# Vision transformer layer on one core: the wavelet tokeniser handled in pieces, with one gate chain and an inverse shared by three engines

## The reference, cut to what matters

```python
img = x[..., 0]                       # 8 images of 256 x 256
details, cur = [], img
for _ in range(3):                    # three Haar analysis levels
    cur, h, v, d = _dwt2(cur)
    details.append((h, v, d))
aw = sigmoid(cur.reshape(B, -1) @ Wa + ba)
rec = cur * aw[:, :, None]
for (h, v, d), (Wd, bd) in zip(reversed(details), [(Wd1, bd1), (Wd2, bd2), (Wd3, bd3)]):
    w = softmax(stack([h, v, d], 1).reshape(B, -1) @ Wd + bd, -1)     # 3 gates of a level
    rec = _idwt2(rec, h * w[:, 0], v * w[:, 1], d * w[:, 2])          # gates broadcast over a band
h = concatenate([cls_tok, rec], axis=1)         # an image row is a token: 257 tokens of 256
h = h + attention_block(layernorm(h))           # linear attention with 16 heads, then an MLP
h = h + moe(layernorm(h))                       # 8 experts, 2 per token
```

## Time and profile before

| what | value |
|---|---|
| median of three runs | 739.04 us (737.57 to 739.18) |
| the profiled execution | 734.85 us |
| its span, first to last instruction | 733.0 us |
| PE busy | 684.5 us, 93% |
| DVE / ACT / POOL busy | 47% / 40% / 39% |
| mean granted TensorE clock | 0.966 |

### The profile page before, as it was taken

How to read it: one execution, slowest core, us unless ns; L and a number is a source line. 1 busy time by engine, 2 the same in 40 slices (tenths; PEclk the granted TensorE clock), 3 DMA queues, 4 the chain that set the end, 5 groups by cost and what they waited for, 6 DMA issues and landing times.

```text
span 733.0 us, 14613 instructions
## 1 busy us (share of the span) xinstructions
PE 684.5 (93%) x4607; PEld 605.7 (83%) x4608; DVE 343.6 (47%) x1029; ACT 293.7 (40%) x762; POOL 289.1 (39%) x324
## 2 busy tenths in 40 slices
PE   0977999999999999999999999999999999999993
PEld 0755888889988877788888788999999999999993
DVE  5493766666532643654566554333333333333330
ACT  0432665466532363444345242333342424333330
POOL 7003677676662353444533332323232323232221
PEclk9978999999959999999999999999999999999997
DMA  9605999700000298011021253221221211122210
GB/s 210 221 2 97 271 303 307 207 0 1 2 0 1 82 377 289 16 45 45 23 81 59 96 183 94 37 43 30 44 34 30 34 34 30 30 36 37 36 22 0
DMA packets 53222, 63.97 MB, mean 87 GB/s; under 512 B 6348, under 2 KB 48768, under 8 KB 53008
## 3 DMA queue, kind: packets, MB, share of 16 engines
q1 hardware_dynamic: 41264, 50.61, 23.7%
q0 software_dynamic: 8112, 9.04, 7.4%
q10 hardware_dynamic: 3808, 3.82, 1.7%
HBM read 31.01 MB, written 31.38 MB: 85 GB/s over the span
## 4 chain that ended last, share of the span: by engine, by line
PE 73%; DVE 9%; SPq 5%; DMA 4%; issue 3%; ACT 2%; POOL 2%; DVEq 0%; POOLq 0%; ACTq 0%
PE bank L1702 70%; SPq L574 3%; DMA arena<-in_L_tok_Wa 2%; PE bank L2209 1%; DVE arena L1032 1%; DMA out_tokens<-h 1%; DMA h<-arena 1%; DVE small L549 1%; POOL small L570 1%; SPq L642 1%; PE bank L1734 1%; POOL arena L764 1%; PE bank L1880 1%; SPq L578 1%; DVE dense L562 1%
## 5 line engine op out<-in xcount | busy, mean ns | idle before, releaser
L1702 PE MATMUL bank<-arena,dense 128*128 (+2 forms) x1408 | 307.0, 389 | 1.1 <-ACT arena L1496 0.8
L1702 PEld LDWEIGHTS bank<-arena,dense 128*128 128x128 f32 (+1 forms) x1408 | 247.2, 193 | 37.1 <-ACT arena L1595 2.9
L1671 ACT ACTIVATE dense<-bank,small 128x128 f32<-128x128 f32 x320 | 91.1, 368 | 182.5 <-PE bank L1702 182.5
L857 POOL DMA_INDIRECT out_tokens<-dense,slot_ids x40 | 77.1, 1928 | 206.1 <-DVE dense L1415 197.4
L1702 PEld LDWEIGHTS bank<-dense 128*128 128x128 f32 x1280 | 149.0, 192 | 3.9 <-DVE dense L1393 2.0
L1702 PE MATMUL bank<-dense 128*128 128x128 f32 x1280 | 149.6, 275 | 1.6 <-DVE dense L1393 1.6
L1702 PE MATMUL bank<-dense,arena 128*128 128x256 f32 (+2 forms) x688 | 105.2, 352 | 1.1 <-ACT arena L1509 0.7
L764 POOL TENSOR_TENSOR arena<-arena 128x512 f32<-128x512 f32 x64 | 80.3, 1277 | 40.7 <-ACT arena L1529 40.7
L1702 PEld LDWEIGHTS bank<-dense,arena 128*128 128x128 f32 (+2 forms) x688 | 81.8, 186 | 16.3 <-issue 4.2
L1595 ACT ACTIVATE arena<-bank,small 128x256 f32<-128x256 f32 x128 | 53.7, 471 | 81.7 <-PE bank L1702 81.5
L1702 PE MATMUL bank<-arena 128*128 128x34 f32 (+7 forms) x756 | 81.8, 301 | 3.1 <-ACT arena L1595 1.6
(11 more groups left out here) (247 smaller groups left out, 580.1 us busy)
## 6 DMA issues: line engine op xcount, KB each, us to landing
routed_rows<-x SPq DMA_DIRECT2D x8, 2385.0 KB, 24.3
arena<-in_L_ffn_w SPq DMA_DIRECT2D x13, 1024.0 KB, 12.5
dense<-routed_rows SPq DMA_DIRECT2D x40, 132.5 KB, 2.1
arena<-in_L_ffn_w ACTq DMA_DIRECT2D x3, 1024.0 KB, 9.4
arena<-in_x SPq DMA_DIRECT2D x4, 512.0 KB, 7.0
arena<-in_L_attn_w SPq DMA_DIRECT2D x2, 1024.0 KB
out_tokens<-h SPq DMA_DIRECT2D x8, 256.0 KB, 2.2
h<-arena SPq DMA_DIRECT2D x13, 128.0 KB
```

The costliest lines, as they stand in the source:

```text
L857: pool.indirect_dma_start(out=sums[:, :], out_offset=bass.IndirectOffsetOnAxis(ap=slot_ids[par][:, 0:1], axis=0), in_=y[par], in_offset=No ...
L1671: act.activation(hT[par][:, k, :], psUP[par][c][:, P * m:P * m + P], ACT.Silu, bias=b1now[par][:, k:k + 1]).then_inc(hT_sb, 1)
L1702: return pe.matmul(out, lhsT, rhs, start=start, stop=stop, **kw)
```

## The change

- **Loads.** ACT's small loads and POOL's 16 wait for the image's last piece (`img_loaded[3]`). The weights of levels 1 and 2 come with 96 rows of half the length, so that one transpose turns two blocks; level 1's have a semaphore of their own.
- **Bands by piece.** DVE makes level 1's bands as each piece of the image arrives. PE turns them piece by piece, in eight units of three blocks, and multiplies in the order 1, 2, 3 of the levels. `picked` and the like are made after the analysis.
- **One gate chain.** `pick`, `total`, the logits and the exponentials are done once for all three levels, after the last dot product.
- **Inverse of level 1.** ACT multiplies the second and third band by their gates. POOL forms the high sums from them, in four instructions. DVE forms the low sums and interleaves, in two half strips of 8 rows, and raises `image_ready` after each.
- **Relayout.** A transfer takes 8 rows of each of an image's 16 strips. A token tile's partition p then holds another row of the image than before, and `ids` and the stores of `h` follow; a store becomes two. SP issues the first halves of images 0 to 2 after the first `image_ready`, then the second halves, then image 3. ACT issues those of images 4 to 7, behind its copies of the weights. POOL issues none.

```diff
@@ ACT, start
+            act.wait_ge(img_loaded[PIECES - 1], 16)
             for dst, src in smalls:
@@ POOL
+            pool.wait_ge(img_loaded[PIECES - 1], 16)
             for hh in range(HEADS):
...
-            pool.wait_ge(image_ready, 1)
-            for b in range(HELPED):
-                relay(pool, b, 1, helped[b])
+            pool.wait_ge(scaled, 2)
+            for part in range(2):
+                for r, op in ((0, ALU.add), (1, ALU.subtract)):
+                    ins = pool.tensor_tensor(hi4[:, 4 * part:4 * part + 4, r, :], level1(det[1][:, 1024:2048], part),
+                                             level1(det[1][:, 2048:3072], part), op)
+                ins.then_inc(hi_ready, 1)
+            pool.wait_ge(image_ready, 2)
@@ relay
-            p0 = STRIPS * b + STRIPS // T * j
-            eng.dma_start(h[:, T * b + j, :], img[p0:p0 + STRIPS // T, :].rearrange("p (r n) -> p r n", r=ROWS)
+            p0, c0 = STRIPS * b, RUN * IMG * j
+            eng.dma_start(h[:, T * b + j, :], img[p0:p0 + STRIPS, c0:c0 + RUN * IMG].rearrange("p (r n) -> p r n", r=RUN)
@@ SP
-            sp.wait_ge(image_ready, 1)
-            for b in range(B):
-                relay(sp, b, 0, relaid[min(b, 4)])
-                if b >= HELPED:
-                    relay(sp, b, 1, relaid[min(b, 4)])
+            for j in range(T):
+                sp.wait_ge(image_ready, j + 1)
+                for b in range(3):
+                    relay(sp, b, j, relaid[b])
+            for b in range(3, ON_SYNC):
+                for j in range(T):
+                    relay(sp, b, j, relaid[min(b, 4)])
...
-                sp.dma_start(sums[bass.ds(g * SEQ + 1, IMG), :].rearrange("(t p) n -> p t n", p=P),
-                             h[:, bass.ds(T * g, T), :]).then_inc(stored[par], 16)
+                for j in range(T):
+                    sp.dma_start(sums[bass.ds(g * SEQ + 1, IMG), :].rearrange("(s t r) n -> s t r n", s=STRIPS, t=T)[:, j, :, :],
+                                 h[:, bass.ds(T * g + j, 1), :].rearrange("p o n -> p (o n)")).then_inc(stored[par], 16)
@@ DVE
-            cur, side, rows = img, IMG, ROWS
-            for lvl in (1, 2, 3):
...
+            for i in range(PIECES):
+                dve.wait_ge(img_loaded[i], 16)
+                analyse(1, img, IMG, ROWS, i, PIECES)
...
-            pick(0)
-            logits_of(0, ((0, 3, 0.25), (4, 8, 0.125)), 2)
...
+            dve.wait_ge(dots_ps, 2)
+            for i in range(2):
+                ins = dve.tensor_tensor(dotted[:, i, :, :], psDots[i].rearrange("p (b s) -> p b s", s=STRIPS),
+                                        own.rearrange("p (o s) -> p o s", o=1).to_broadcast([P, B, STRIPS]), ALU.mult)
...
             link(merge(3))
-            pick(1)
             spread(2, 0, gsc[:, 12:13])
-            logits_of(1, ((0, 3, 0.5),), 1)
             link(merge(2))
             dve.wait_ge(c_ps, 1)
             dve.tensor_copy(c_xT, psT[:, 0:KD]).then_inc(c_done, 1)
...
-            spread(1, 8, gsc[:, 17:18])
-            merge(1).then_inc(image_ready, 1)
+            for part in range(2):
+                r0, m0 = 4 * part, 1024 * part
+                for r, g in ((0, gate[:, 8:9]), (1, gsc[:, 14:15])):
+                    ins = dve.scalar_tensor_tensor(out=rows4[:, r0:r0 + 4, r, :], in0=d0[:, r0:r0 + 4, :], scalar=g,
+                                                   in1=base[:, r0:r0 + 4, :], op0=ALU.mult, op1=ALU.add)
+                link(ins)
+                dve.wait_ge(hi_ready, part + 1)
+                for two, op in ((0, ALU.add), (1, ALU.subtract)):
+                    ins = dve.tensor_tensor(o2[:, m0:m0 + 1024, two], lohi[:, m0:m0 + 1024],
+                                            lohi[:, 2048 + m0:2048 + m0 + 1024], op)
+                ins.then_inc(image_ready, 1)
@@ ACT
+            act.wait_ge(gates_ready, 1)
+            for k in (1, 2):
+                d = det[1][:, 1024 * k:1024 * (k + 1)]
+                act.activation(d, d, ACT.Identity, scale=gate[:, 8 + k:9 + k]).then_inc(scaled, 1)
...
+            act.wait_ge(image_ready, 2)
+            for b in range(ON_SYNC, B):
+                for j in range(T):
+                    relay(act, b, j, relaid[4])
```

More of the change, by code:

```diff
@@ L52 @@
 TURNED_FIRST = 4
+RUN = ROWS // T
 BANDS = 3 * STRIPS
@@ L56 @@
 PIECES = 4
-HELPED = 3
+ON_SYNC = 4
 class Chain:
@@ new lines, in _ @@
+            levels = gate[:, 0:12].rearrange("p (l k) -> p l k", k=4)[:, :, 0:3]
+            dve.wait_ge(totals_ready, 1)
+            for i, c0, c1, scale in ((0, 0, 3, 0.25), (0, 4, 8, 0.125), (1, 8, 11, 0.5)):
+                ins = dve.scalar_tensor_tensor(out=gate[:, c0:c1], in0=psTotal[i][:, c0 - 8 * i:c1 - 8 * i],
+                                               scalar=scale, in1=bd[:, c0:c1], op0=ALU.mult, op1=ALU.add)
+            link(ins)
+            link(dve.tensor_reduce(gsc[:, 0:3], levels, AX_X, ALU.max))
@@ L1463, in bands_out @@
             def bands_out(s):
-                dst = det_units[turn_order[s]][1]
+                dst = det_units[s][1]
                 act.wait_ge(detT_ps, s + 1)
                 act.copy(dst, psTurn[s % 4][0:dst.shape[0], 0:dst.shape[1]]).then_inc(detT_sb, 1)
-            for s in range(7):
+            for s in range(2):
                 bands_out(s)
+            for u in range(4):
+                weights_out(u)
+            for s in range(2, 4):
+                bands_out(s)
+            for u in range(4, 6):
+                weights_out(u)
@@ L1469, in _ @@
+            for s in range(4, 11):
+                bands_out(s)
+            levels = gate[:, 0:12].rearrange("p (l k) -> p l k", k=4)[:, :, 0:3]
             act.wait_ge(logits_ready, 1)
             act.activation(gate[:, 7:8], gate[:, 7:8], ACT.Exp, scale=-1.0)
-            coarse = gate[:, 0:8].rearrange("p (l k) -> p l k", k=4)[:, :, 0:3]
-            act.activation(coarse, coarse, ACT.Exp).then_inc(exps_ready, 1)
-            for s in range(7, 9):
-                bands_out(s)
-            act.wait_ge(logits_ready, 2)
@@ L1476, in _ @@
-            act.activation(gate[:, 8:11], gate[:, 8:11], ACT.Exp).then_inc(exps_ready, 1)
+            act.activation(levels, levels, ACT.Exp).then_inc(exps_ready, 1)
+            act.wait_ge(gates_ready, 1)
+            for k in (1, 2):
+                d = det[1][:, 1024 * k:1024 * (k + 1)]
+                act.activation(d, d, ACT.Identity, scale=gate[:, 8 + k:9 + k]).then_inc(scaled, 1)
             def turned_out(u):
@@ L1728, in turn_bands @@
             def turn_bands(s):
-                lvl, dst, blocks = det_units[turn_order[s]]
-                pe.wait_ge(bands_ready, turn_order[s] // 2 + 1 if lvl == 1 else 4 * lvl)
+                lvl, dst, blocks = det_units[s]
+                pe.wait_ge(bands_ready, 4 * (s // 2) + 3 if lvl == 1 else 4 * (PIECES + lvl - 1) - (1 if lvl == 2 else 0))
                 after(pe, detT_sb, s - 3)
@@ L1754, in dot_bands @@
                 return ins
[L1756 to L1768 removed]
+            turn_bands(0)
+            turn_bands(1)
+            pe.wait_ge(wd3_loaded, 16)
+            for u in range(4):
+                turn_weights(u)
+            turn_bands(2)
+            turn_bands(3)
+            pe.wait_ge(wd_loaded, 16 * 3)
+            turn_weights(4)
+            turn_weights(5)
+            pe.wait_ge(wdT_sb, 4)
+            dot_bands(0)
+            dot_bands(1)
+            turn_bands(4)
+            turn_bands(5)
+            dot_bands(2)
+            dot_bands(3)
+            turn_bands(6)
+            turn_bands(7)
+            dot_bands(4)
+            dot_bands(5)
             dot_bands(6)
             dot_bands(7).then_inc(dots_ps, 1)
[L1771 to L1779 removed]
+            turn_bands(8)
+            turn_bands(9)
+            pe.wait_ge(wdT_sb, 6)
+            dot_bands(8)
+            dot_bands(9)
+            turn_bands(10)
+            dot_bands(10).then_inc(dots_ps, 1)
+            pe.wait_ge(dots_ready, 1)
+            for i, (pattern, n) in enumerate(((picked, 8), (band_sum, 4))):
+                ins = mm(psTotal[i][:, 0:n], dotted[:, i, :, :].rearrange("p b s -> p (b s)"), pattern)
+            ins.then_inc(totals_ready, 1)
             pe.wait_ge(c_norm, 1)
```

228 lines of the change are left out of this document (105 added, 123 removed).

## The result

The changed kernel takes 750.19 us (median of four, 749.35 to 753.18). The kernel before took 739.11 beside it (737.57 to 740.10). The ratio is 1.016, 95% interval 1.0125 to 1.0196: 11 us slower. The forecast was 738.8 with a range up to 743.0, so it was wrong. The profiled execution took 750.12, its span is 748.0 and the mean granted clock 0.949.

The account below looks back on a forecast made before the run. The start of ACT's copy of image 0's tokens (64.08 us) was taken as the bound; moving it by -0.5 and adding +0.3 elsewhere gave -0.2 us, so 738.8 from the median 739.04, range 735.0 to 743.0.

Parts of the forecast that it names:

- step 9: ACT's lane before the copy of image 0's tokens: eight relay issues at 0.7 us, 5.6 in all, copy at 63.6 instead of 64.08.
- second rival: ACT's eight relay issues last as long as transfers drain, 12 us instead of 5.6: copy at 70, time 745; chance 0.12.
- Step 1: Start of ACT and PE: holding small loads back brings the image at 9.5 us, ACT copies from 17.3, replacing 18.65.
- fourth rival: The image doesn't come earlier: last piece stays at 12.4, ACT starts 2.9 us later, time 741.7; chance 0.07.
- Step 2: PE from the third weight unit at 18.7 to the last dot product: 13.5 us, ending at 32.2, bounds 31.3 to 33.7.
- Steps 3 and 4: Gates, then levels 3 and 2 on DVE: gates at 36.8, level 3 to 38.9, level 2 alone 3.3 us, to 42.2.
- Step 5: DVE's level 2 beside POOL's four instructions: DVE loses 3.5 us, bounds 0 and 5.1; `c_xT` is copied at 45.9.
- first rival: POOL costs DVE nothing at level 2: `c_xT` at 42.4, L1496 4.0 us earlier, time 735.1; chance 0.31 with its milder form.
- Step 6: Level 1 on DVE without the high rows: 7.2 us, image whole at 53.1 against 52.96.
- Step 7: Relayout of image 0: one 128 KB transfer lands in 2.7 us, bounds 2.2 and 6.6; tokens' lane ends at 59.0, 3.9 earlier.
- Step 8: PE's lane, attention weights and class token: starts on `c_xT`, ends at 61.4, 2.1 us later than before; L1818 done at 62.5.
- Elsewhere: Rest of the kernel, chiefly the stores of `h` split into two issues: +0.3 us, bounds 0 and 1.3.

## Why the prediction was wrong

**What failed is step 9**, "I take 0.7: 5.6 us". The eight issues took 18.6, 13 more. ACT's lane ended ahead of them at 57.9 (58.0 forecast), so this one term explains all of the 12.5 us between the forecast 63.6 and 76.08, and -0.2 + 12.5 = +12.3 is near the measured +11.1. The nearness is partly luck: the delay grew by 3 us more behind the copy, and the forecast was worked out on an execution 4.3 us quicker than its kernel's median. The mechanism is that of the second rival, "ACT's relays block it", with padding sharing the engines. It had a chance of 0.12 and even its price, 12 us and 745, was too low. It was priced with relays that drain alone in the kernel before (1.61); but from 56.8 on the engines were never alone. The 0.64 and 0.75 on which the 0.7 rests were the first three and the first two issues of their queues, and the first one is 0.70 here too. SP's third took 3.56 us already in the kernel before. Beside padding the second takes 1.8, the third 2.2, and the later ones 1.8 to 3.5.

In step 9 the Trainium skill, "DMA: Bandwidth & Descriptors", section "Why a DMA increments its semaphore by 16 and not by 1", was read as: 16 engines instead of 8, so "ACT isn't held". The first half agrees with the runs: relays alone fill 0.82 of the engines' share where those before filled 0.45, though the rate rises only from 90 to 138 GB/s, so that a relay drains in 0.6 of the time and not in half. The second half didn't follow, because padding fills the same engines. The same page of the Trainium skill, section "Issuing engines are not separate DMA queues", says that transfers of all issuing engines interleave, and that a second issuer only saves issue time, "usually small relative to the DMA itself". The first agrees: ACT's relays land 2.5 us apart beside SP's padding and 0.90 apart without. The issue time is not small here, 18.6 us of it on the engine that PE waits for.

**Step 1** gave the right time for the wrong reason. First copy forecast at 17.3, found at 16.67; image in at 9.5, found at 9.96. But the hold-back, which the step credits, costs: without it the first copies of bands are at 10.03, those of weights at 15.03 instead of 17.41, and the time is 4.6 us shorter than with the hold-back (731.47 against 736.11, both with the relays on SP). Step 1 left out that SP's weights land at 12.9, so that PE stood waiting for ACT and not for the image. The fourth rival took for granted that the image's arrival is what counts.

**Step 2**: 32.2 forecast, 31.7 found, and that is luck. PE's own rate was indeed the unknown, but the step reads it wrongly: the 0.23 and 0.165 us a block aren't "at the same granted clock". The first record of the clock in the trace of before is at 28.1 us; the 0.23 at 24.16 lies ahead of it, where PE runs at its slow rate, and the 0.165 behind it. In the changed kernel's trace the record comes at 22.5. In the nine other traces with the same start it comes at 24.6 to 28.7, and the dot products end at 32.6 to 35.3, in five of the nine beyond the step's bound of 33.7.

**Steps 3 and 4**: gates at 36.2 (36.8 forecast), level 2 from 38.3 (38.9).

**Step 5**: 3.9 lost (3.5 forecast), `c_xT` at 45.64 (45.9). The first rival is refuted. What the step took from the Trainium skill, "SBUF — State Buffer", section "Who interferes with whom", agrees with the run without POOL's instructions: 0.44 us for each of the four instead of 1.4. Of the step's own two places only L905 has two inputs in SBUF; L1032 has one.

**Step 6**: the image is whole at 53.2 (53.1). **Step 7**: landing 3.1 (2.7), DVE's tokens ready at 59.6 (tokens' lane 59.0 forecast). **Step 8**: PE's lane ends at 60.9 (61.4), L1871 is done at 61.5, not released by DVE, as said. **Elsewhere**: +0.3 forecast for the split stores of `h`, nothing found.

So image 0's tokens are transposed at 61.5 instead of 64.1, 2.5 us earlier, where the steps have 62.5, and then ACT gives 14.5 away. With the relays on SP the same steps give 3 us in the medians, a gain.

## What to carry to other kernels

A DMA issue is an instruction of the engine that makes it. Here, from the fourth of a burst on, ACT's issues went at the pace at which its queue drained, 0.9 us a relay alone and 2.5 beside the padding that filled the DMA engines. Price a burst of issues by its later members and by the traffic of that moment, not by the first ones, and put it on an engine on which nothing waits behind it. Before holding a load back so that another comes earlier, look at whether the consumer of that other was idle at all, and what the late issues will then stand in front of.

## What the runs showed of the hardware

- The length of the n-th issue of a 128 KB transfer depends on those ahead in its queue: 0.70, 1.8, 2.2, 2.9 with 2385 KB stores on another queue beside it, 0.70, 0.70, 0.89, 1.33 without. Over eight issues the pace is that of the landings, 2.5 us and 0.9.
- Two inputs in SBUF on DVE beside POOL's instructions of the same kind: 1.4 us instead of 0.44 each, one let in per POOL instruction of 1.38.
- At the start of every execution profiled, PE ran for a time at the rate of 1.2 GHz, although the stretch views print 1.00: they have no record there. The records begin at 17.9 to 28.7 us, and at that moment the median step from one matmul to the next falls from 0.21 to 0.10 or 0.11 us, as between stretches recorded at 0.50 and at 1.00. Among kernels with the same start this moves the gates from 36.2 to 39.4. PE had worked for 3.7 us (14.1 to 17.9) or for 8.7 (15.3 to 24.0) by then; the rows don't show what decides it.
